# A graph layer over 16 pairs of graphs, written out by hand for five engines: every engine's list of tasks in a new order, and parts of the projection and the un-sorting between quarters of gathers

## The reference

```
mask = (adj > 0)
xj_proj = x @ W1a                      # W1a, W1b: upper and lower half of W1
diff[j, k] = x[j] - x[k]
h[j, k]  = relu(xj_proj[j] + diff[j, k] @ W1b + b1)      # 256 x 256 x 192 per graph
hm[j]    = sum over k of mask[j, k] * h[j, k]
out      = layernorm(x + hm @ W2 + deg * b2)             # deg[j] = number of neighbours
```

## Time and profile before

| | |
|---|---|
| runs shown | 254.0, 254.54, 255.02 us, median 254.54 |
| profiled execution, first to last instruction | 253.0 us |
| PE busy | 239.2 us, 95%, 2813 matmuls |
| DVE busy | 230.0 us, 91%, 810 instructions |
| ACT busy | 214.8 us, 85%, 636 instructions |
| POOL busy | 133.1 us, 53%, 288 instructions |
| DMA | 18.21 MB, mean 72 GB/s, about 350 GB/s in the first 19 us |
| mean granted TensorE clock | 0.986 |

### The profile page before, as it was taken

How to read it: one execution, slowest core, us unless ns; L and a number is a source line. 1 busy time by engine, 2 the same in 40 slices (tenths; PEclk the granted TensorE clock), 3 DMA queues, 4 the chain that set the end, 5 groups by cost and what they waited for, 6 DMA issues and landing times. The chain is left out here.

```text
span 253.0 us, 9425 instructions
## 1 busy us (share of the span) xinstructions
PE 239.2 (95%) x2813; PEld 190.5 (75%) x2813; DVE 230.0 (91%) x810; ACT 214.8 (85%) x636; POOL 133.1 (53%) x288
## 2 busy tenths in 40 slices
PE   7968999999999999999999999999999999999990
PEld 2536687878887978878877878878887879777870
DVE  4797799999999999999999999999999999979853
ACT  2396999898989999898989989898989898988820
POOL 1415252565555574655554564655655555454834
PEclk9997999999999999999999999999999999999997
DMA  6992003501312203031212203031310110000001
GB/s 196 349 352 87 1 3 127 146 4 43 106 45 51 98 22 106 26 106 41 105 41 76 69 20 99 27 105 44 104 45 25 41 29 17 4 21 3 25 21 51
DMA packets 10552, 18.21 MB, mean 72 GB/s; under 512 B 1296, under 2 KB 7696, under 8 KB 10512
## 3 DMA queue, kind: packets, MB, share of 16 engines
q1 hardware_dynamic: 10512, 17.73, 21.7%
HBM read 15.63 MB, written 2.10 MB: 70 GB/s over the span
## 5 line engine op out<-in xcount | busy, mean ns | idle before, releaser
L1287 PE MATMUL ring<-hot,vh 128*128 128x128 bf16 (+9 forms) x768 | 115.8, 254 | 0.9 <-ACT ring L869 0.4
L1287 PE MATMUL ring<-hot,vl 128*128 128x128 bf16 (+9 forms) x768 | 113.9, 251 | 0.0
L1737 DVE SCALAR_TENSOR_TENSOR sums<-ring,sums 128x256 f32<-128x256 f32 (+14 forms) x304 | 104.9, 375 | 8.7 <-PE ring L1287 4.0
L1287 PEld LDWEIGHTS ring<-hot,vh 128*128 128x128 f16 (+1 forms) x768 | 61.0, 102 | 18.9 <-issue 7.9
L874 ACT COPY ring<-u_sb 128x144 f32<-128x144 f32 (+13 forms) x256 | 65.2, 302 | 9.6 <-DVE sums L1737 7.9
L1287 PEld LDWEIGHTS ring<-hot,vl 128*128 128x128 f16 (+1 forms) x768 | 62.2, 103 | 2.8
L631 POOL TENSOR_TENSOR vl<-vf,vh 128x384 f16<-128x384 f32 x32 | 34.4, 1075 | 49.2 <-ACT vf L839 32.3
L869 ACT COPY ring<-u_sb 128x512 f32<-128x512 f32 (+1 forms) x80 | 45.0, 565 | 0.9 <-PE ring L1111 0.4
L1710 DVE TENSOR_SCALAR hot<-slotT 128x944 bf16<-128x944 f16 (+6 forms) x112 | 28.5, 267 | 0.0
L685 POOL TENSOR_TENSOR sums<-taken,sums 128x512 f32<-128x512 f32 x16 | 20.3, 1272 | 11.7 <-ACT taken L891 11.7
L790 ACT CAST maskT<-bx 128x512 bf16<-128x512 f32 x32 | 18.4, 583 | 8.8 <-PE bx L1139 7.7
(11 more groups left out here) (117 smaller groups left out, 470.8 us busy)
## 6 DMA issues: line engine op xcount, KB each, us to landing
adj_sb<-adj SPq DMA_DIRECT2D x16, 512.0 KB, 3.5
x_sb<-x_pairs SPq DMA_DIRECT2D x16, 128.0 KB, 2.3
xT_sb<-xT SPq DMA_DIRECT2D x16, 128.0 KB, 2.4
x_all<-x SPq DMA_DIRECT2D x4, 512.0 KB, 8.1
out<-o_sb SPq DMA_DIRECT2D x16, 128.0 KB, 1.7
wts<-weights SPq DMA_DIRECT2D x1, 417.0 KB, 4.8
cst_general<-general SPq DMA_DIRECT2D x1, 256.0 KB, 2.7
cst_half<-half SPq DMA_DIRECT2D x1, 137.0 KB, 3.2
```

Source lines behind the costliest of these rows:

```text
L1287: return eng.matmul(to if part == "main" else to[g * HT:g * HT + HT], values, selection, start=False, stop=final, skip_group_check=True)
L1737: eng.scalar_tensor_tensor(out=to, in0=view(pair, part, unit, piece), scalar=0.0, in1=to, op0=ALU.max, op1=ALU.add).then_inc(added[part], 1)
```

## The change

All five engines keep their tasks, units, banks, buffers and waits, except SP, whose list isn't touched. The order of the lists of POOL, ACT, PE and DVE is new: at the start, in the body and at the end. Three PE functions get a range, so that a part of them can be issued, with the waits on the first part and the semaphore on the last:

```diff
-            def project(pair):
-                if pair.general:
+            def project(pair, first=0, end=3 * NT):
+                if first == 0:
...
-                for t in range(NT):
+                for step in range(first, end):
+                    t, g = divmod(step, 3)
...
-            def unsort_y(pair):
+            def unsort_y(pair, first=0, end=TILES):
...
-            def gather(pair, part, unit):
+            def gather(pair, part, unit, first=0, end=TILES):
...
+                steps = steps[2 * first:2 * end]
...
-                last.then_inc(gathered[part], 1)
+                if end == TILES:
+                    last.then_inc(gathered[part], 1)
```

POOL's body:

```diff
             def body(pair, has=always):
-                older, old, new, second, third = pair.at(-2), pair.at(-1), pair.at(1), pair.at(2), pair.at(3)
-                if has(1):
-                    residual(new)
+                elder, older, new, second = pair.at(-3), pair.at(-2), pair.at(1), pair.at(2)
+                if has(0):
+                    low_v(pair, 1)
+                if has(1):
+                    degree_bias(new)
+                    corrections(new)
+                if has(0):
+                    residual(pair)
                 if has(2):
-                    corrections(second)
+                    degrees(second)
+                if has(0):
+                    add_taken(pair, 0)
                 if has(-2):
-                    scale(older)
...
+                    moments(older)
+                if has(-3):
+                    scale(elder)
+                if has(-2):
+                    centre(older)
+                if has(1):
+                    low_v(new, 0)
```

DVE's start:

```diff
             sort_key(Pair(0, 0))
+            prepare_weights()
             ranks(Pair(0, 0))
-            prepare_weights()
             permutation(Pair(0, 0))
             first_max()
+            make_ident()
+            masks(Pair(0, 1))
             ranks_above(Pair(0, 0))
+            masks(Pair(0, 2))
             weight_top()
             count_given(Pair(0, 0))
             first_scales()
             select(Pair(0, 0), 0)
+            count_masks(Pair(0, 1))
             select(Pair(0, 0), 1)
-            masks(Pair(0, 1))
-            make_ident()
             select(Pair(0, 0), 2)
-            count_masks(Pair(0, 1))
...
```

PE's end (the gathers of pair 15 and `unsort_y` of pair 14 stand ahead of it as before; `add_over` moves up to the first gathers of pair 15):

```diff
             unsort_y(Pair(0, 14))
+            project(Pair(0, 15))
+            unsort_y(Pair(0, 15))
             keep_busy_last(7)
-            project(Pair(0, 15))
-            add_over()
             keep_busy_last(2)
-            unsort_y(Pair(0, 15))
```

More of the change, by code:

```diff
@@ L940, in body @@
                 if has(0):
+                    seed(pair, "main", 0)
                     seed(pair, "tail", 0)
@@ new lines, in project @@
+                if end == 3 * NT:
+                    last.then_inc(y_ready, 1)
+            def unsort_y(pair, first=0, end=TILES):
+                if first == 0:
+                    eng.wait_ge(y_copied, pair.n + 1)
+                    eng.wait_ge(permT_copied, pair.n + 1)
+                for c in range(first, end):
+                    g, t = divmod(c, NT)
+                    last = eng.matmul(bx3[:, (TILES + c) * O:(TILES + c + 1) * O], permT[pair.side][:, c, :],
+                                      y_sb[:, t * 2 + g, :], start=True, stop=True)
+                if end == TILES:
+                    last.then_inc(z_ready, 1)
@@ L1335, in body @@
                 new, second, third = pair.at(1), pair.at(2), pair.at(3)
-                if has(0):
-                    gather(pair, "main", 6)
-                if has(1):
-                    turn_perm(new)
-                if has(2):
-                    number_slots(second, 0)
-                    number_slots(second, 1)
                 if has(1):
                     gather(new, "main", 0)
-                if has(2):
-                    sort_x(second)
-                    excess_tail(second)
-                if has(1):
                     gather(new, "tail", 0)
@@ L1369, in body @@
                     gather(new, "main", 4)
+                    gather(new, "tail", 2)
+                    gather(new, "tail", 3)
                 if has(2):
@@ L1372, in body @@
                 if has(1):
-                    gather(new, "main", 5)
+                    gather(new, "main", 5, 0, 2)
                 if has(3):
@@ L1376, in body @@
                 if has(1):
-                    gather(new, "tail", 2)
-                    gather(new, "tail", 3)
+                    gather(new, "main", 5, 2, 4)
+                    gather(new, "main", 6, 0, 2)
                 if has(3):
                     turn_masks(third, 1)
+                if has(1):
+                    gather(new, "main", 6, 2, 4)
+                if has(2):
+                    turn_perm(second)
+                if has(3):
+                    number_slots(third, 0)
+                    number_slots(third, 1)
+                    sort_x(third)
+                    excess_tail(third)
             keep_busy(14)
@@ L1847, in body @@
                 if has(-1):
-                    add(old, "tail", 5)
+                    add(old, "main", 6)
+                    add(old, "tail", 6)
+                if has(1):
+                    count_given(new)
                 if has(0):
@@ L1851, in body @@
                 if has(-1):
-                    add(old, "tail", 6)
+                    add(old, "tail", 7)
                 if has(0):
                     select(pair, 10)
-                if has(1):
-                    count_given(new)
-                if has(-1):
-                    add(old, "tail", 7)
-                if has(-3):
-                    inverse_deviation(elder)
-                if has(2):
-                    count_masks(second)
                 if has(-1):
@@ L1865, in body @@
                     add(old, "main", 7)
+                    reduce_small(old)
+                    add(old, "main", 8)
+                if has(-3):
+                    inverse_deviation(elder)
+                if has(-1):
                     add(old, "tail", 9)
-                    add(old, "main", 8)
-                    reduce_small(old)
+                if has(3):
+                    masks(third)
+                if has(-1):
                     add(old, "main", 9)
+                if has(-2):
+                    statistics(older)
+                if has(-1):
+                    add_small(old)
+                if has(2):
+                    count_masks(second)
                 if has(0):
@@ L2001, in _ @@
             add(Pair(0, 15), "main", 1)
+            select(Pair(0, 15), 8)
+            add(Pair(0, 15), "tail", 3)
             add(Pair(0, 15), "main", 2)
```

475 lines of the change are left out of this document (235 added, 240 removed).

## The result

| | median of the runs | profiled span | pairs 2 to 15, from hidden_u_tail to hidden_u_tail |
|---|---|---|---|
| kernel before | 254.44 us (254.0 to 255.02) | 253.0 | 182.9 us, 14.07 a pair |
| changed kernel | 282.97 us (282.6 to 285.31) | 280.9 | 201.8 us, 15.53 a pair |

The ratio is 1.1146, with a 95% interval of 1.1101 to 1.119. 263.3 us was predicted, in a range of 254.0 to 268.0: the sign was right, the size was not, and the time lies outside the range.

The account below looks back on a forecast made before the run. PE was taken as the first bound, DVE second, 0.55 us under it; in the new order DVE sets the loop. 254.5 + 6.2 (start) + 3.6 (loop) - 1.0 (end) = 263.3 us, range 254.0 to 268.0.

Parts of the forecast that it names:

- The start, +6.2 (5 to 7.5): Kernel start: DVE stands at masks(2) for adj of pair 2 until 17.4, delaying count_given(0); 6.2 us slower, between 5 and 7.5.
- ten busy us behind that as before: Pair 1, behind hidden_u(1): the work after the late start was taken to last ten busy us, unchanged.
- The new stall, 0.8 us a pair: Loop: GpSimd's add_taken gets in behind select 2 and holds DVE's select 3; 0.8 us a pair lost.
- 0 to 0.4: Loop: GpSimd's centre and scale of older pairs meet DVE's select 4 and 8, costing 0 to 0.4 us.
- The bound of 1.5 for the whole: Loop: upper bound on the new DVE stalls together, 1.5 us; the lower was 0 if the phases miss.
- The loop without stalls, 13.6: Loop without new stalls: DVE needs 13.5 us and sets the pace, 13.6 a pair with what stays of waits.
- The forecast of 6.1 us off: Loop without new stalls: 13 pairs each 0.47 us shorter, 6.1 us off.
- PE's 13.43 and DVE's 13.5: Loop work per pair in the new order: PE 13.43 us, from 13.64, with waits taken out; DVE 13.5 us.
- the one at unsort_y: PE, main 3: unsort_y matmuls between gather quarters hide weight loads, 0.15 us off a pair.
- as much again: PE: project in parts around hidden_u_tail and main 1 saves as much as unsort_y's 0.15 us a pair.
- the rivals' 253.6 and 249.4: Both have the loop gain: 253.6 us with the start's cost (17%), 249.4 with start only +2 (7%).
- The end, -1.0: Kernel end: earlier project(15), no fillers before unsort_y, and 0.5 us of DVE idle time recovered; 1.0 us off (-2 to 0).

Follow-up runs that it names:

- experiment 1: Changed kernel with the start's masks of pair 2 moved back behind count_given of pair 1 on DVE: 274.75 us, ratio 1.0753 to the kernel before.
- Experiment 5: Changed kernel with one GpSimd wait added, so that low_v of the new pair's first graph starts after DVE's select 8: 273.24 us, ratio 1.0767.
- experiment 2: Changed kernel with GpSimd's add_taken cut to one column in place of 512: 272.97 us, ratio 1.0724.
- the repaired order: Changed kernel, masks moved back, count_masks behind select 3, add_taken waiting for select 3, scale and degrees after it, centre and low_v for select 8: 258.54 us, ratio 1.0144.
- experiment 13: The repaired order with copy_slots of the new pair's second graph moved directly behind the first's on ScalarE: 257.48 us, ratio 1.0122.
- experiment 10: The repaired order with TensorE's parts of projection and un-sorting put together again: 259.53 us, ratio 1.0187.

## Why the prediction was right in sign and wrong in size

The time was missed by 19.7 us. By the cut at hidden_u_main 15.0 of them are the loop (18.6 for 3.6), 2.4 the start with pair 1 (8.6 for 6.2) and 1.7 the end (+0.7 for -1.0); 0.6 is the difference between spans and medians.

**The start, +6.2 (5 to 7.5).** Right in place and mechanism: adj at 17.4, given at 18.32 for 18.3, hidden_u_tail(1) 6.0 later. By experiment 1 the whole of it is 7.2 us of span, because it also lengthens pair 1. The first pair was counted as "ten busy us behind that as before"; it was not. DVE comes to select 3 and 4 while GpSimd does scale_inputs (31.66 to 32.9), add_taken (32.89, 1.42) and four more operations in one block, to 36.5, and later to masks while GpSimd does low_v (38.23, 0.92) and degrees:

```profile
33.18 2.10 DVE L1738 TENSOR_SCALAR hot<-slotT 128x944 bf16<-128x944 f16 x2
...
38.41 1.29 DVE L1550 TENSOR_SCALAR mask<-adj_sb 128x1024 bf16<-128x1024 f32 x1
```

The two selects take 0.40 and 0.35 alone and the masks 0.69: 2.0 us of holds, in a pair that the prediction's sum left out. With the masks moved back neither is there, and the stretch (11.57 us) is no longer than in the kernel before.

**The new stall, 0.8 us a pair: this is the step that failed.** Its first part was right: select 0 first, add_taken in behind select 2, select 3 held, 0.8 foreseen and 0.75 measured. The prediction then gave "0 to 0.4" for centre and scale and took none of it (0.39 was measured on select 5), and did not look for low_v(p+1, 0) at all, which stands behind centre on GpSimd and takes 0.97 us. It holds sort_key for 0.65. sort_key is an operation on two tensors like ranks_above, which the prediction counted among those that can be held. Experiment 5 gives low_v's part as 0.70 a pair, experiment 2 that of add_taken as 0.73 (net of what the shifted holds changed), and the repaired order, which takes away nearly all of them, gives 1.30 a pair. The bound of 1.5 for the whole was too low for the same reason: 1.8. The rest of the loop's sum was near: 13.55 of DVE's own work, 1.79 of holds and 0.19 idle make 15.53, where the prediction had 13.5, 0.8 and 0.05.

**The loop without stalls, 13.6: not reached either.** With the holds gone the order takes 14.23, and 14.14 with one more wait removed, where the kernel before takes 14.07. The forecast of 6.1 us off rested on PE's 13.43 and DVE's 13.5. DVE's busy time in experiment 13 is 176.6 us in 13 pairs, 13.58, so that sum holds; but 0.56 a pair stays in which DVE is not busy. The waits that the profile names in it are for PE, for gathers (2.1 us from 65 to 220) and for excess_main (1.3). The prediction let both engines come within 0.1 of the larger sum, and in none of these orders do they: the kernel before had 0.35 of DVE's time idle, the repaired one 0.51. Of the two gains that PE's interleaving was given, the one at unsort_y was there in size (1.53 for 1.67 us, foreseen 0.15 off). The other, "as much again" for project, was not: 4.25 us with the parts and without (experiment 10). What there was of it was worth 1 us in the repaired order, nothing under DVE's pace, and less than nothing in the order before. So the rivals' 253.6 and 249.4, which rest on 13.6, had too much of the chance.

**The end, -1.0: wrong in sign.** From hidden_u_main(15) on it is +0.7. project(15) starts 0.05 us behind add_small (271.41, the add ending at 271.36), where it was 0.4, as foreseen. But add_small itself comes no earlier: it ends 23.0 us behind hidden_u_main(15), against 22.5 before, so the 0.5 that DVE was to give is lost instead. And unsort_y(15) has no fillers ahead of it any more, only the wait of 1.04 us before project and one of 0.46 before itself. The granted clock falls from 2.4 to 1.2 GHz at 273.1, and its eight half products take 1.97 us instead of 1.00. No run shows whether fillers would have kept the clock up.

**The sum of what was measured:** 8.6 + 18.6 + 0.7 = 27.9 on the 253.0 of span (by hidden_u_tail 6.0 + 3.3 + 18.9 - 0.3). The loop's 18.9 is 13 x 1.46: 1.62 more of DVE's busy time, 199.42 against 178.42, and 0.16 less of its idle time. The holds are 1.8 us a pair in three instructions, and now and then one of ranks_above (957 ns) or select 6 (975). That they show as 1.62 is in part because the kernel before had small holds of its own on select 0, 0.1 a pair; the rest of that gap was not traced.

What stays open: why DVE's sum comes later at the end, why experiment 1 reaches hidden_u_main(2) 0.7 us later than the kernel before although given(0) is only 0.1 later, and which wait keeps the repaired order from 13.6. No version that was run beats the kernel before; the best is experiment 13 at 1.2% above it.

## What to carry to other kernels

When two engines that disturb each other are reordered, write down for every operation of the one what the other does beside it, all the way round the loop; a single overlooked pair cost 0.7 us here thirteen times over. When a hold is cured by a wait, look first for who reads what the waiting instruction writes: here the wait was free only where a stretch of work that is not held (count_masks) lay between the two. A second stream that is interleaved into a first may shorten their sum (here 0.14 of 1.67 us for one, nothing for the other) and delays the first one's end, so it pays only where nobody waits for that end. And when stretches of two orders are compared, the mark has to have the same work ahead of it in both: hidden_u_tail made the end look 0.3 us shorter, when it was 0.7 longer.

## What the runs showed that was not expected

- The hold goes both ways. DVE's select, sort_key, ranks_above, permutation, masks or count_rest waits for the end of the GpSimd operation beside it; and while such instructions follow one another on DVE, GpSimd's add_taken takes 1.97 instead of 1.27 us. Adds from PSUM, start_sums and the reduce of count_masks were not held in these traces (0.94 and 1.10 us beside the extra operation, 1.21 beside add_taken).
- The price of a hold is set by when the GpSimd operation ends, not by the size of the held instruction: sort_key has 72 elements a partition and went from 0.22 to 0.94 us.
- Adding a wait to a half idle engine made the kernel 9.7 us faster, and an extra operation of 1 us on it, 3.0 and 2.6 us slower, though GpSimd was busy for only 53% of the time before.
